# An attention and mixture-of-experts layer on one core: a shorter expert choice, q and k stacks filled from SBUF to SBUF in three buffers, and the maxima 24 steps ahead

## What is computed

```python
q = (x @ Wq.T + bq).reshape(B, T, H, hd).transpose(0, 2, 1, 3)      # k, v alike
zq = q @ V; zk = k @ V; zv = v @ V
att = softmax(einsum('bhqr,bhkr->bhqk', zq, zk) / sqrt(rank))
y = (einsum('bhqk,bhkr->bhqr', att, zv) @ U.T).transpose(0, 2, 1, 3).reshape(B, T, D)
x = layernorm(x + y @ Wo.T + bo)
gate_probs = softmax(x @ gate_w.T)
topk_scores, topk_idx = top_k(gate_probs, 2)
topk_scores = topk_scores / sum(topk_scores)                        # into combine[t, e]
h = relu(einsum('td,ehd->teh', x, w1) + b1)
out = einsum('ted,te->td', einsum('teh,edh->ted', h, w2) + b2, combine)
x = layernorm(x + out)
```

## Time and profile before

| | us |
|---|---|
| timed runs, median of 3 (lowest, highest) | 1321.52 (1320.30, 1324.97) |
| the profiled execution | 1309.61 |
| its span, first to last instruction | 1307.8 |

### The profile page before, as it was taken

The page is one execution under the profiler, slowest core; times in us unless marked ns, Lnnn a source line. Parts: engine busy times, 40 slices in busy tenths (PEclk is TensorE's granted clock), DMA queues, the critical chain, the costliest instruction groups (busy, mean ns, idle before and its releaser), DMA issues. The chain is left out here.

```text
span 1307.8 us, 24700 instructions
## 1 busy us (share of the span) xinstructions
PE 1072.2 (82%) x7709; PEld 508.8 (39%) x7709; DVE 1016.2 (78%) x2339; ACT 894.1 (68%) x1113; POOL 583.3 (45%) x780
## 2 busy tenths in 40 slices
PE   3478998879798887979788797977744999999977
PEld 1132222222122222213222222312224999999962
DVE  2588898879797887979779797978335888888855
ACT  1057887668586675858667675756844999999937
POOL 1123415344343533434443343523234777777745
PEclk9999999889898988989999898989986999999989
DMA  3832233341313324131342413220002222222236
GB/s 73 261 115 77 82 104 80 87 123 46 107 52 97 109 63 122 50 99 52 97 118 55 122 50 99 56 84 26 10 21 71 69 70 70 69 69 70 69 133 271
DMA packets 108790, 114.31 MB, mean 87 GB/s; under 512 B 19816, under 2 KB 82066, under 8 KB 108704
## 3 DMA queue, kind: packets, MB, share of 16 engines
q1 hardware_dynamic: 99104, 92.10, 25.0%
q0 software_dynamic: 8448, 16.93, 3.7%
q10 hardware_dynamic: 1152, 4.19, 0.8%
HBM read 64.45 MB, written 48.44 MB: 86 GB/s over the span
## 5 line engine op out<-in xcount | busy, mean ns | idle before, releaser
L853 DVE TENSOR_REDUCE row_max<-score_ps 128x2 f32<-128x1024 f32 x512 | 614.4, 1218 | 126.6 <-PE score_ps L594 69.2
L687 ACT ACTIVATE probs<-score_ps 128x1024 f32<-128x1024 f32 x512 | 519.7, 1024 | 223.5 <-PE score_ps L578 149.5
L556 PE MATMUL av_ps<-probs,v_one 128*9 128x512 f32 x2048 | 287.3, 635 | 9.8 <-ACT probs L687 9.1
L594 PE MATMUL score_ps<-k_stack,q_stack 64*128 64x512 bf16 x1024 | 209.7, 407 | 98.9 <-issue 48.8
L578 PE MATMUL score_ps<-q_stack,k_stack 64*128 64x512 bf16 x1024 | 207.7, 404 | 54.2 <-DVE row_max L853 49.4
L578 PEld LDWEIGHTS score_ps<-q_stack,k_stack 64*128 64x128 bf16 x1024 | 49.0, 93 | 355.5 <-DVE row_max L853 198.0
L1140 ACT ACTIVATE w_cur<-experts 128x1156 f32 x136 | 158.5, 1167 | 41.9 <-PEq L414 22.0
L1236 POOL DMA_INDIRECT y_d<-y_out,place x136 | 137.1, 1008 | 43.5 <-issue 43.5
L923 POOL DMA_INDIRECT routed_d<-rows,slot_i x128 | 125.1, 977 | 47.7 <-issue 39.3
L388 POOL TENSOR_TENSOR max_parts<-neg_max,zeros 32x128 bf16<-32x128 f32 x32 | 14.3, 446 | 295.0 <-DVE neg_max L700 295.0
L1097 PE MATMUL up_ps<-xt_sb,w_cur 128*128 128x128 f32 x1088 | 145.0, 277 | 0.0
(11 more groups left out here) (191 smaller groups left out, 1176.0 us busy)
## 6 DMA issues: line engine op xcount, KB each, us to landing
k_stack<-k_stack_d SPq DMA_DIRECT2D x64, 256.0 KB, 3.4
q_stack<-q_stack_d SPq DMA_DIRECT2D x64, 256.0 KB, 4.2
x_rows_sb<-routed_d SPq DMA_DIRECT2D x136, 65.0 KB
q_stack_d<-q_parts SPq DMA_DIRECT2D x32, 192.0 KB, 2.8
k_stack_d<-k_parts SPq DMA_DIRECT2D x32, 192.0 KB, 2.8
x_in<-L_attn_x SPq DMA_DIRECT2D x16, 256.0 KB, 6.4
q_stack_d<-q_parts SPq DMA_DIRECT2D x32, 128.0 KB, 2.5
k_stack_d<-k_parts SPq DMA_DIRECT2D x32, 128.0 KB, 2.6
```

Source lines behind the costliest of these rows:

```text
L556: last = nc.tensor.matmul(av_ps[32 * g:32 * g + V_COLS, :], v_one[n.parity][:, kb, HG * hg + g, :], probs[:, (2 * j + g // 2) % P_RING, g ...
L594: last = nc.tensor.matmul(score_ps[(2 * s + 1) % 3 if cur else s % 2][:, a, :], q_stack[n1.parity][at, c, g * P:(g + 1) * P], k_stack[n1.p ...
L687: nc.scalar.activation(probs[:, s % P_RING, :, :], score_ps[2 * s % 3][:, :, :], ACT.Exp).then_inc(S["exp_done"], 1)
L853: nc.vector.tensor_reduce(row_max[:, s // (STEPS // 2), :, s % (STEPS // 2)], score_ps[(2 * s + 1) % 3 if cur else s % 2][:, :, :], AX.X, ...
```

## The change

- **Stacks.** No copies through DRAM. `fill` writes each part from `q_parts` or `k_parts` straight to a place of the stack, 64 KB from 64 partitions into 8: 24 DMAs a batch, and three buffers of each stack. Places are now six for parts and three rows of maxima; there is no blank, so products run over 51 rows (scores) or 48 (maxima) of each half. The rows of ones are written once in setup. In the first body ACT issues eight of the 24; later SP issues all, the last six behind the row copies of the maxima.
- **Lag.** The maxima run 24 steps ahead of the exps (`LAG`), not 32.
- **Order of the small jobs.** x at step 1, q at 13, k at 15, the ranks at 5, maxima half 1 at 9 and half 0 at 25; `emptied` derives their waits.
- **Engines.** ACT negates the maxima, copies v (whose bias is folded into `bo_b` in setup) and copies the logits; POOL computes `shift` and writes the rows' places by iota.
- **Choice.** Logits are compared instead of probabilities; the two weights come from one exp of the gap: 16 operations for 21, and five for ten in `route`.
- **Scatters.** Two, four and two at three places of POOL's body.
- **Weights and barrier.** The experts' weights are loaded only once batch 0's stack is full. Setup no longer waits for stores.

```diff
-POS = 8
-MAX_POS = 5
-ROWS = POS * R
+LAG = 24
+ROWS = 64
+SCORE_ROWS = 6 * R
+MAX_ROWS = 3
+Q_SLOTS = ((0, 0), (0, 1), (0, 2), (1, 3), (1, 4), (2, 5))
+K_SLOTS = ((0, 0), (1, 1), (2, 2), (0, 3), (1, 4), (0, 5))
+SP_FIRST = 2
+SP_EARLY = 3
...
-                    for n in range(2):
-                        for stack_d, row, tile in ((q_stack_d[n], MAX_POS, blank), (q_stack_d[n], POS - 1, blank),
-                                                   (k_stack_d[n], MAX_POS, k_ones), (k_stack_d[n], POS - 1, blank)):
...
-                    sp.wait_ge(blanks_stored, 16 * 16)
+                    for n in range(3):
+                        for a in range(2):
+                            row = a * ROWS + SCORE_ROWS
+                            sp.dma_start(k_stack[n][row:row + MAX_ROWS, :, :], k_ones[:, :].unsqueeze(1).to_broadcast([MAX_ROWS, PAIRS, T])).then_inc(ones_stored, 16)
...
-                    sp.wait_ge(pads_stored, 16)
...
+                    pe.wait_ge(act_setup, 2)
+                    nc.tensor.matmul(misc_ps[:, 0:P], bv_hr[:, :], wo_t[:, :], start=True, stop=True).then_inc(pe_setup, 1)
...
+                    nc.vector.tensor_tensor(bo_b[:, :], misc_ps[:, 0:P], bo_b[:, :], ALU.add).then_inc(dve_setup, 1)
...
+            def fill(queue, n, stack, parts, slots):
+                for part, slot in slots:
+                    for a in range(2):
+                        row = a * ROWS + slot * R
+                        queue.dma_start(stack[n.third][row:row + R, :, :], parts[a * ROWS:(a + 1) * ROWS, part, :]).then_inc(stack_filled[n.third], 16)
...
+            def maximum_at(b, s):
+                m = b.c * STEPS + s + LAG
+                return m if 0 <= m < B * STEPS else None
...
-                            if s == 5 and proj:
+                            if s == 1 and proj:
                                 pe.wait_ge(x_loaded[n2.parity], n2.count_parity(16, 16))
...
-                            if s == 23 and nxt:
+                            if s == 25 and nxt:
                                 pe.wait_ge(S["red_done"], n1.count(STEPS, STEPS // 2))
...
+                            if s == 17 and is_first(b):
+                                act.wait_ge(S["split_done"], 2)
+                                fill(act, n2, k_stack, k_parts, K_SLOTS[SP_FIRST:])
...
-                            nc.vector.scalar_tensor_tensor(shift[:, :], mean_var[:, :, 0], -1.0, rstd[:, :],
-                                                           ALU.mult, ALU.mult).then_inc(S["shift_ready"], 1)
...
                         if proj and not is_first(b):
+                            split_q(nc.gpsimd, pool, n2)
                             split_k(nc.gpsimd, pool, n2)
                         if prev2:
+                            scatter(p2, 2, 6)
                         if nxt:
                             split_max(n1, 0)
                         if prev2:
+                            scatter(p2, 6, 8)
...
-                            store_parts(q_stack_d[n2.parity], q_parts, Q_PLACES)
+                            wait(sp, S["st_done"], b.count(STEPS, 0))
+                            fill(sp, n2, q_stack, q_parts, Q_SLOTS)
                             sp.wait_ge(S["split_done"], n2.count(2, 2))
-                            store_parts(k_stack_d[n2.parity], k_parts, K_PLACES)
+                            fill(sp, n2, k_stack, k_parts, K_SLOTS[:SP_FIRST if is_first(b) else SP_EARLY])
                         if nxt:
                             max_rows(n1, 0)
-                        if proj:
-                            sp.wait_ge(S["parts_stored"], n2.count(16 * STORES, 16 * STORES))
-                            stacks(n2, 0)
-                            stacks(n2, 1)
-                            wait(sp, S["sm_done"], n1.count(STEPS, 3 * GROUP))
-                            stacks(n2, 2)
+                        if proj and not is_first(b):
+                            fill(sp, n2, k_stack, k_parts, K_SLOTS[SP_EARLY:])
+                        if is_first(b):
+                            sp.wait_ge(stack_filled[n2.third], n2.count_third(16 * FILLS, 16 * FILLS))
```

More of the change, by code:

```diff
@@ L43, in __init__ @@
         self.parity = c % 2
+        self.third = c % 3
     def __add__(self, d):
@@ L155, in build_layer @@
             rstd = asb("rstd", [P, QT])
+            minus_mean = asb("minus_mean", [P, QT])
             shift = asb("shift", [P, QT])
-            rows = [[asb(f"rows{n}_{w}", [P, QT, ROW]) for w in range(2)] for n in range(2)]
+            rows = [asb(f"rows{n}", [P, 2, QT, ROW]) for n in range(2)]
             x1_t = asb("x1_t", [P, T])
@@ L397, in split_q @@
                 queue.wait_ge(S["q_sb"], n.count(1, 1))
-                wait(queue, S["parts_stored"], n.count(16 * STORES, 0))
+                if n.c > 0:
+                    queue.wait_ge(stack_filled[(n + -1).third], (n + -1).count_third(16 * FILLS, 16 * FILLS))
                 wait(queue, S["split_done"], n.count(2, 0))
@@ L639, in scale_out, with neg @@
                                 wait(act, scattered[n.parity], n.count_parity(8 * 16, 0))
-                            nc.scalar.activation(rows[n.parity][0][:, t, 0:D], res[:, t, :], ACT.Identity, bias=shift[:, t:t + 1],
+                            nc.scalar.activation(rows[n.parity][:, 0, t, 0:D], res[:, t, :], ACT.Identity, bias=shift[:, t:t + 1],
                                                  scale=rstd[:, t:t + 1]).then_inc(S["x1_ready"], 1)
+                        def neg(n, half):
+                            act.wait_ge(S["maxt_done"], n.count(2, half + 1))
+                            wait(act, S["maxsplit_done"], n.count(2, half - 1))
+                            nc.scalar.activation(neg_max[half][:, :], misc_ps[0:HALF, 0:P], ACT.Copy, scale=-1.0).then_inc(S["negmax_sb"], 1)
                         def copy_expert(e):
@@ L819, in body @@
+                            if s <= 4 and prev2:
+                                for k in (2 * s + 6, 2 * s + 7):
+                                    choose(p2, k)
+                            if 6 <= s <= 8 and prev2:
+                                for k in (2 * s - 12, 2 * s - 11):
+                                    if k < SLOT_STEPS:
                                         route(p2, k)
@@ L895, in split_max, with scatter @@
                                   lambda k: n.count(6, 3 * half + k), S["maxsplit_done"])
-                        if cur:
-                            split_max(b, 1)
+                        def scatter(n, first, last):
+                            for k in range(first, last):
+                                w, t = divmod(k, QT)
+                                nc.gpsimd.indirect_dma_start(
+                                    routed_d, bass.IndirectOffsetOnAxis(ap=slot_i[n.parity][:, w, t:t + 1], axis=0),
+                                    rows[n.parity][:, w, t, :], None).then_inc(scattered[n.parity], 16)
+                        if prev2:
+                            wait(pool, scattered[p2.parity], p2.count_parity(8 * 16, 0))
+                            nc.gpsimd.iota(rows[p2.parity][:, :, :, D + 1].bitcast(i32), pattern=[[1, 2], [2 * P, QT]],
+                                           base=2 * T * p2.c, channel_multiplier=2).then_inc(S["place_out"], 1)
                         if prev:
@@ L903, in body @@
                                                     ALU.add).then_inc(S["xbo_ready"], 1)
-                        if proj and not is_first(b):
-                            split_q(nc.gpsimd, pool, n2)
+                        if cur:
+                            split_max(b, 1)
+                        if prev2:
+                            pool.wait_ge(S["place_out"], p2.count(1, 1))
+                            pool.wait_ge(S["top_step"], p2.count(TOP_STEPS, TOP_STEPS))
+                            pool.wait_ge(S["slot_step"], p2.count(SLOT_STEPS, SLOT_STEPS))
+                            pool.wait_ge(S["copied"], p2.count(1, 1))
+                            scatter(p2, 0, 2)
                         if prev:
```

459 lines of the change are left out of this document (183 added, 276 removed).

## The result

| | us |
|---|---|
| changed kernel, median of 4 runs (lowest, highest) | 1305.16 (1301.29, 1311.14) |
| before, median of 4 runs beside them | 1322.94 (1320.30, 1324.97) |
| ratio, with its 95% interval | 0.987 (0.983 to 0.992) |
| the profiled execution, and its span | 1301.29, 1299.2 |

What follows compares the result with a forecast made beforehand. DVE was taken as nearly the bound, PE just behind, with slow batches waiting on held completions. Terms summed to -95: 1309.6 - 95 = 1214.6, times 1.0091 gives 1226 us; own range 1200 to 1256, overall 1176 to 1288.

Steps and rivals of the forecast that it cites:

- Setup, -8.0: Setup barrier: SP's stores no longer waited for, so the loop's first transposes start at 14.2 instead of 22.27; gain 8.0 us.
- first maxima at 26.2: Sign in the new timeline: the first maxima of the loop were to start at 26.2 us.
- First fills, -1.6: From q's first stores to the first maxima: 16 fills at 0.62 us plus 2.1, 12.0 instead of 13.6; gain 1.6 us.
- the third rival: Fills on SP's queue move slowly, each writing only 8 partitions; at 1.2 us a fill 1362 us; chance 0.14.
- X: Price per fill on SP's queue; the change would lose all its gain of 95 us at X = 1.09 us.
- Prologue of 24, -6.5: Before the first scores: eight maxima less save 10.5 us, PE waits 4 for the experts' weights; gain 6.5 us.
- Scatters, -98 and +13: Attention batches 2 to 14: parting the scatters removes 7.5 us of wait a body, 98; 13 put back for the four.
- Four just do [reach it]: POOL's group of four scatters just reaches the held completions, which begin as the fourth is issued; 1.0 us a batch.
- x late, +34: PE's x_in transposes wait for a load issued behind SP's row copies and fills: 2.4 us in 14 bodies, 34.
- a sign but gave no price: the row copies: Sign that would show the forecast wrong altogether: maxima rows landing after step 0 or 16; no size given.
- DVE relief, -27: Every batch: 3.8 us off DVE makes PE the bound, 47.6 against 49.3 us; gain 1.7 x 16 = 27.
- The end, -2: Behind the last exp: ten fewer small operations in series, 2 us less.

Runs made afterwards that it cites:

- fast fills: Changed kernel with each fill writing the same 64 KB to eight partitions six apart instead of eight neighbours: 1242.9 us beside 1221.4 for the kernel before.
- session V: Kernel before with its eight scatters of a batch in four pairs, nothing else: 1220.4 us against 1317.7, ratio 0.925, where holds occurred.
- 49.5 with pairs: Kernel before with its eight scatters in four pairs, where nothing was held: 1217.1, 1216.7 and 1217.0 us beside 1221, 1220 and 1220.
- the kernel with pairs: Changed kernel with fills six partitions apart, x loaded ahead of the fills and the four scatters parted into two pairs: 1211.4 us beside 1318.9.
- both kernels with pairs: Kernel before with only its scatters in four pairs (1217.0 us), and changed kernel with spread fills, x loaded ahead and paired scatters (1211.4 us).
- The load on DVE: The 1211 us kernel with 12 small multiplications into unread tiles put on DVE in every batch: 1219.0 us, period 49.3 to 50.0.
- fills spread and x ahead: Changed kernel with fills six partitions apart and batch b+3's x loaded ahead of the fills, run of four scatters kept: 1268.1 us beside 1318.9.
- the changed kernel with pairs: Changed kernel with only its group of four scatters parted into two pairs, one each side of k's split: 1277.6 us beside 1221.4, ratio 1.045.
- both together: Changed kernel with fills six partitions apart, x loaded ahead of them and scatters in pairs: 1211.4 us beside 1318.9, no remote wait.

## Why the prediction was wrong, point by point

The time, 1305, lies above both ranges of the prediction, 1200 to 1256 and 1176 to 1288. Three steps failed: that a run of four scatters hardly reaches the hold (priced at 1.0 us a batch, measured 4.4), that a fill goes at a store's rate (0.62 us, measured 0.93, which also made the row copies late), and that what comes off DVE shortens the batch (27 us in all; the periods show some 3).

- **Setup, -8.0: right.** Transposes at 14.28, forecast 14.2. (The sign that I gave for the next step, first maxima at 26.2, does not follow from the terms: they give 43.4 - 9.6 = 33.8. Measured was 44.68.)
- **First fills, -1.6: wrong, +9.2.** I took a fill at a store's 0.62 us since "in form, size and source it is the same". The destination was what differed, and it set the rate: 0.93 us in a body. I had both ends (0.4 and 2.1) and the third rival worked out to X, but gave it 0.14.
- **Prologue of 24, -6.5: wrong, -1.0.** Eight maxima less did come. Against them stand 5.4 us for the weights (I took 4) and 3.5 for the first scores, which wait for row copies. The slow fills are not the cause of that wait: it is 3.5 us with fast fills too. The shorter lead of the maxima is the likely cause, and no run tests it.
- **Scatters, -98 and +13: the cause right, the cure half.** Taking the hold away is worth 97 us (session V), and a batch without it was put at 49.3 and is 49.3 (49.5 with pairs). The step that failed is "Four just do [reach it]", priced at 1.0 us a batch. The row that I had, the hold from the fourth scatter on, said that four are enough to start it; only its length behind the fourth shrinks. Measured: 4.4 us a body, wait and half clock, 57 us.
- **x late, +34: right in size, hidden in part.** 31.4 us where nothing is held and the fills are fast; 17.0, 18.3 and 28.5 us in three traces of the changed kernel, and there beside other waits.
- **What I named as a sign but gave no price: the row copies.** The third rival asked when x would land behind 24 fills. The six row copies stand behind 18 and are wanted at step 0: they are the first to be late, 3.8 us a body at X = 0.93, well under the 1.09 at which I had let that rival decide. I had followed the moved load past the queue, but not what had stayed in it.
- **DVE relief, -27: mis-sized.** I counted 3.8 us off DVE; its busy time in a batch fell by 3.0 in the changed kernel and by 2.0 to 2.3 in the kernel with pairs. I took `shift` at 0.89 us, but all except 0.15 of it was time beside a POOL operation, and with pairs `tied` loses as much. The periods, of both kernels with pairs and without remote waits in the loop, fall from 49.5 to 49.3: 0.2 a batch, some 3 us in all, which also holds the moved small jobs. The load on DVE shows more, some 0.7 of 1.2 us. I took PE plus 3.3 us of idle time as the bound, 47.6; the batch with pairs has PE busy for 44.9 of 49.2 us, so 4.3 us of idle time stayed. I put that down to the step's turn of PE, ACT and the three banks; no run isolates it.
- **The end, -2: did not come** (+0.3).

The costs don't add: hold and late rows take the same place. A period is 49.3 us without either, mostly 53 to 55 with one, and hardly more with both. So taking away the late transfers alone (fills spread and x ahead, with holds: 1268), or the hold alone (the changed kernel with pairs, session without holds: 1278), leaves much of the loss; both together give 1211.

## What to carry to other kernels

Here a transfer's rate went with the partitions that it wrote: before replacing a path through DRAM by copies into a few neighbouring partitions, measure one such copy, and then ask of everything behind them in the queue when it is wanted, not only of what the change moved. A wait that is taken away uncovers the one that it hid; give an edit its worth only together with what is next. A small operation that a profile shows at several times its usual length may be waiting beside another engine: its time doesn't leave with it. And where a forecast rests on a wait that a trace shows, check in a second session that it is the kernel's own.

## What the runs showed of the hardware

- In some sessions PE's completions reach ACT and DVE late when four or more indirect scatters follow one another at 1.27 us, seen from 3.9 us after the first. ACT and DVE then wait up to 2.9 us behind runs of four, and up to 5.9 us (ACT) and 7.7 us (DVE) behind runs of eight. No wait stands behind a pair in the two traces with pairs from such sessions. In other sessions the same kernel shows none of it: 1221 against 1321 us. What makes a session the one or the other is open; so is the mechanism, and so is whether three in a run are held.
- Copies of 64 KB from 64 partitions into 8: neighbours 71 GB/s, six apart 158 GB/s. The latter were issued on two queues every 0.68 and 0.78 us, which by my estimate would allow some 180, so what sets the 158 is open. Two queues at once did not raise the 71.
- A DVE operation of 0.15 to 0.19 us takes 1.1 us when it starts inside a POOL operation on 128x512, and ends with it.
